# Last image layer and the dense end part with channels on partitions, layers written out on TensorE

## The reference

```python
x = coords @ fc0_w + fc0_b                       # 3 -> 32 channels
for sw, cw, cb in (four layers):
    x1 = spectral_conv(x, sw)                    # rfft2, 20 x 20 modes mixed by sw, irfft2
    x2 = einsum('bchw,oc->bohw', x, cw) + cb     # 1x1 convolution
    x = gelu(x1 + x2)
x = gelu(x @ fc1_w + fc1_b)                      # 32 -> 64 channels, per pixel
return (x @ fc2_w + fc2_b)[..., 0]               # 64 -> 1
```

## Time and profile before

| | |
|---|---|
| median of 3 runs | 4450.04 us (4443.79 to 4450.76) |
| the profiled execution | 4450.9 us, span 4448.7 us |
| mean granted TensorE clock | 0.754 |
| PE busy | 3744.6 us (84%) |
| PEld busy | 3132.7 us (70%) |
| DVE busy | 2504.3 us (56%) |
| ACT busy | 549.9 us (12%) |
| POOL busy | 740.6 us (17%) |
| image block: first transpose of half 1 to last copy into `ho` | 30.0 to 1840.7 us |

### The profile page before, as it was taken

The page is one execution under the profiler, slowest core; times in us unless marked ns, Lnnn a source line. Parts: engine busy times, 40 slices in busy tenths (PEclk is TensorE's granted clock), DMA queues, the critical chain, the costliest instruction groups (busy, mean ns, idle before and its releaser), DMA issues. The chain is left out here.

```text
span 4448.7 us, 109537 instructions
## 1 busy us (share of the span) xinstructions
PE 3744.6 (84%) x44268; PEld 3132.7 (70%) x44268; DVE 2504.3 (56%) x8138; ACT 549.9 (12%) x1173; POOL 740.6 (17%) x1900
## 2 busy tenths in 40 slices
PE   6999999999999999697656566687998878859587
PEld 5898988769989887454424455687997778857444
DVE  4454545145455452223756888888787887852413
ACT  0101011310010112211211110101001000001011
POOL 1000000000000000000002434334343332332021
PEclk9999999999999999777855555555555555556589
DMA  1010000000000000100003110111000000021111
GB/s 37 16 17 2 16 2 16 2 6 16 2 16 16 2 1 2 25 0 4 0 10 91 32 35 29 31 29 31 26 25 32 22 29 24 22 75 46 21 39 27
DMA packets 189736, 96.97 MB, mean 22 GB/s; under 512 B 139463, under 2 KB 172535, under 8 KB 188632
## 3 DMA queue, kind: packets, MB, share of 16 engines
q1 hardware_dynamic: 183574, 84.19, 8.1%
q10 hardware_dynamic: 4626, 7.39, 0.4%
q0 software_dynamic: 1280, 2.10, 0.2%
HBM read 76.11 MB, written 15.96 MB: 21 GB/s over the span
## 5 line engine op out<-in xcount | busy, mean ns | idle before, releaser
L349 PEld LDWEIGHTS im_acc<-im_cwt,im_chan 128*128 128x128 f32 x2048 | 268.7, 191 | 123.0 <-issue 117.3
L468 ACT ACTIVATE im_a<-im_acc 128x512 f32<-128x512 f32 x256 | 152.9, 597 | 1376.7 <-PE im_acc L349 1376.7
L204 POOL DMA_DIRECT2D image_rows<-im_ho x16 | 9.6, 603 | 1761.2 <-DVEq L459 1761.2
L445 DVE COPY im_chan<-im_ring 128x512 f32<-128x512 f32 x192 | 132.8, 692 | 286.8 <-PE im_ring L296 286.8
L346 PE MATMUL im_acc<-im_u,im_e 97*128 97x512 f32 x512 | 265.3, 599 | 7.6 <-DVE im_u L439 7.6
L349 PE MATMUL im_acc<-im_cwt,im_chan 128*128 x2048 | 270.1, 274 | 0.0
L258 PE MATMUL im_ring<-im_d,im_a 128*128 128x128 f32 (+1 forms) x2048 | 242.5, 281 | 19.1 <-issue 12.9
L258 PEld LDWEIGHTS im_ring<-im_d,im_a 128*128 128x128 f32 x2048 | 239.5, 198 | 22.1 <-issue 18.5
L1641 PE MATMUL sc_ps<-H,sc_cols 128*128 128x128 f32 x768 | 231.2, 457 | 11.9 <-POOL H L1528 11.5
L439 DVE COPY im_u<-im_ring 80x512 f32<-80x512 f32 x256 | 171.6, 685 | 118.8 <-PE im_ring L290 118.8
L406 DVE COPY im_half_t<-im_ring 128x480 f32<-128x480 f32 x192 | 168.5, 903 | 116.5 <-PE im_ring L258 116.5
(11 more groups left out here) (394 smaller groups left out, 7460.3 us busy)
## 6 DMA issues: line engine op xcount, KB each, us to landing
sc_g_row<-mem_g_rows_dram SPq DMA_DIRECT2D x96, 256.0 KB, 3.5
im_wbd<-in_c_mix_dram SPq DMA_DIRECT2D x32, 400.0 KB, 6.1
sc_w_row<-mem_w_rows_dram SPq DMA_DIRECT2D x192, 64.0 KB, 2.5
sw_g_all<-sw_gates SPq DMA_DIRECT2D x8, 768.0 KB
mem_hist_h_dram<-sc_hist_h ACTq DMA_DIRECT2D x6, 512.0 KB, 3.0
mem_hist_dz_dram<-sc_hist_dz ACTq DMA_DIRECT2D x6, 512.0 KB, 3.7
mo_hist_dz<-mem_hist_dz_dram SPq DMA_DIRECT2D x8, 384.0 KB, 6.4
mo_hist_h<-mem_hist_h_dram SPq DMA_DIRECT2D x8, 384.0 KB, 6.5
```

The costliest lines, as they stand in the source:

```text
L349: mm = MM(acc[:, p % 2, m:512:4], chan[:, p % 2, m * 128:(m + 1) * 128], cwt[:, bass.ds(l, 1), :].rearrange("p a c -> p (a c)"), start=Fal ...
L468: nc.scalar.activation(a[:, g, :, :].rearrange("p c (w x) -> p (c w) x", x=32)[:, :, p * 4:p * 4 + 4], acc[:, p % 2, :].rearrange("p (c m) ...
```

## The change

- In the last layer of each half (l = 3) the operands of the row inverse swap roles: slices of `u` with a step of 4 are the stationary operand (four times), and the first 128 columns of constants `e2` are the moving one. The convolution swaps too: `cwt[l]` is stationary, `chan` is moving with 512 columns. `acc` then holds channels and column index on partitions, in the layout that the end part needs; ScalarE reads it in the order "(m c)" and writes `a` as before.
- In the end part the transposes, their fills and VectorE's copies are gone. The first dense layer reads `a` itself as moving operand, through an access pattern of 4 x 128 elements in which neighbours are 32 elements apart. `FC_FILLS` goes from 40 to 8.
- On TensorE the loop over the layers is written out in the code, so every wait and address there is a constant. VectorE keeps its loop over four layers. ScalarE loops over three and has the fourth written out.

```diff
-        FC0_FILLS, LAYER_FILLS, FC_FILLS = 4 * 9, 4 * 8 + 10 + 4 * 21, 4 * 10
+        FC0_FILLS, LAYER_FILLS, FC_FILLS = 4 * 9, 4 * 8 + 10 + 4 * 21, 4 * 2
...
-                    with pe.Fori(0, NL) as l:
+                    for l in range(NL):
...
-                                MM(acc[:, p % 2, :], e2[0:97, :], u[:, p, :, :].rearrange("p o w -> p (o w)"), start=True, stop=True, skip_group_check=True)
-                                have(f.base + turned[p])
-                                for m in range(4):
-                                    mm = MM(acc[:, p % 2, m:512:4], chan[:, p % 2, m * 128:(m + 1) * 128],
-                                            cwt[:, bass.ds(l, 1), :].rearrange("p a c -> p (a c)"), start=False, stop=True, skip_group_check=True)
+                                if l == NL - 1:
+                                    for m in range(4):
+                                        MM(acc[:, p % 2, m * 128:(m + 1) * 128], u[:, p, :, :].rearrange("p o w -> p (o w)")[:, m:512:4], e2[0:97, :], start=m == 0, stop=True, skip_group_check=True)
+                                    have(f.base + turned[p])
+                                    mm = MM(acc[:, p % 2, :], cwt[:, l, :], chan[:, p % 2, :], start=False, stop=True, skip_group_check=True)
+                                else:
...
-                            turn_activations(f, g, 4 * q)
                             pend = []
                             for p in range(4):
-                                if p < 3:
-                                    turn_activations(f, g, 4 * q + p + 1)
-                                have(start + p + 1)
+                                pixels = a[:, g, :, :].rearrange("p c (w x) -> p (c w) x", x=32)[:, :, (4 * q + p) * 4:(4 * q + p + 1) * 4].rearrange("p j m -> p m j")
                                 for v in range(2):
...
-                                    MM(acc[:, v, :], fc1[:, v, :], chan[:, p % 2, :], start=True, stop=True).then_inc(acc_full, 1)
+                                    MM(acc[:, v, :], fc1[:, v, :], pixels, start=True, stop=True).then_inc(acc_full, 1)
...
-                            for p in range(4):
-                                V.tensor_copy(chan[:, p % 2, :], drain(f)).then_inc(drained, 1)
...
+                    with act.Fori(0, NL - 1) as l:
+                        layer(l, "p (c m) -> p c m")
+                    layer(NL - 1, "p (m c) -> p c m")
```

More of the change, by code:

```diff
@@ L218, in second_layer @@
                 if p + v == 0:
-                    pe.wait_ge(drained, start + 4 + 1)
+                    pe.wait_ge(drained, start + 1)
                 pe.wait_ge(acc_read, SEEN + n + 1)
@@ L222, in second_layer @@
                     col = v * 32 + p * 4 + m
-                    mm = MM(ring[:, (start + 4) % RING, col:col + 17:16], gl[:, v, m * 128:(m + 1) * 128], fc2[:, :], start=True, stop=True)
+                    mm = MM(ring[:, start % RING, col:col + 17:16], gl[:, v, m * 128:(m + 1) * 128], fc2[:, :], start=True, stop=True)
                 return mm
@@ L345, in _ @@
                                 pe.wait_ge(acc_read, SEEN + n - 1)
-                                MM(acc[:, p % 2, :], e2[0:97, :], u[:, p, :, :].rearrange("p o w -> p (o w)"), start=True, stop=True, skip_group_check=True)
-                                have(f.base + turned[p])
-                                for m in range(4):
-                                    mm = MM(acc[:, p % 2, m:512:4], chan[:, p % 2, m * 128:(m + 1) * 128],
-                                            cwt[:, bass.ds(l, 1), :].rearrange("p a c -> p (a c)"), start=False, stop=True, skip_group_check=True)
+                                if l == NL - 1:
[4 more added lines that the diff above has]
+                                else:
+                                    MM(acc[:, p % 2, :], e2[0:97, :], u[:, p, :, :].rearrange("p o w -> p (o w)"), start=True, stop=True, skip_group_check=True)
+                                    have(f.base + turned[p])
+                                    for m in range(4):
+                                        mm = MM(acc[:, p % 2, m:512:4], chan[:, p % 2, m * 128:(m + 1) * 128], cwt[:, l, :], start=False, stop=True, skip_group_check=True)
                                 mm.then_inc(acc_full, 1)
@@ L463, in _, with layer @@
                 for half in range(2):
-                    with act.Fori(0, NL) as l:
+                    def layer(l, order):
                         for g in range(NGRP):
@@ L467, in _ @@
                                 act.wait_ge(acc_full, half * HALF_ACC + l * LAYER_ACC + g * PH + p + 1)
-                                nc.scalar.activation(a[:, g, :, :].rearrange("p c (w x) -> p (c w) x", x=32)[:, :, p * 4:p * 4 + 4], acc[:, p % 2, :].rearrange("p (c m) -> p c m", m=4), ACT.Gelu).then_inc(acc_read, 1)
+                                nc.scalar.activation(a[:, g, :, :].rearrange("p c (w x) -> p (c w) x", x=32)[:, :, p * 4:p * 4 + 4], acc[:, p % 2, :].rearrange(order, m=4), ACT.Gelu).then_inc(acc_read, 1)
+                    with act.Fori(0, NL - 1) as l:
+                        layer(l, "p (c m) -> p c m")
+                    layer(NL - 1, "p (m c) -> p c m")
                     for n in range(4 * PH * 2):
```

## The result

| | before | after |
|---|---|---|
| median | 4448.35 us (4443.79 to 4450.76, 4 runs) | 4637.98 us (4631.60 to 4646.78, 4 runs) |
| span of the profiled execution | 4448.7 us | 4632.4 us |
| mean granted TensorE clock | 0.754 | 0.723 |

What follows compares the result with a forecast made beforehand. TensorE's own sequence in the image network was taken as the bound. End part -53, written-out layers -26 and strided reads 0 gave -79 us, from 4450 to 4371 us; range 4360 to 4402, main case 4362 to 4380 (64%).

Steps and rivals of the forecast that it cites:

- The strided moving operand, "I take zero": End part's first dense layer: reading with a step of 32 elements costs nothing; upper end +74 us on 256 passes.
- Stride halves the rate: Rival, 8%: each moving pass of the first dense layer takes 0.86 instead of 0.43 us, +110 us, 4481 us.
- `u` with a step of 4 as weights, "I take zero": Last layer's row inverse: strided weight loads stay hidden at no cost; upper end 36 us, by VectorE's factor of 1.68.
- The clock, "1 us left": End parts: of 12 us lost to clock falls at quarter borders, nearly all goes with transposes and wait; 1 us left.
- Clock and fetch stay: Rival, 15%: clock falls come from two-column passes (+11 us) and new code bodies stall when fetched (+13 us): 4380 to 4395.
- Layers written out: TensorE's six layer borders: without the loop's branches 27.3 us of branch and clock loss should go; -26 us taken.
- The swapped roles: Last layer's row inverse and convolution: 1.75 us an item before and after (0.89 + 0.86), no change over 64 items.
- The write of PSUM with a step of 4: Last layer's accumulator: writing without stride instead of with stride 4 was put at zero.
- the gelu's other order: Last layer's gelu on ScalarE: reading PSUM in another order was taken as zero; even twice the time shows only 1.2 us.
- Removing transposes and copies: End parts: sixteen quarters of 14.26 us, 228.2 against 282.06 us; -53.9 us at full clock, -53 us as the term.
- a moving pass over 0.5 us: Sign in the end part's first dense layer: the forecast is wrong if a moving pass takes over 0.5 us.
- the clock in the end parts, the third: Sign in the end parts: the forecast is wrong if the clock still falls at every second border of quarters.

Runs made afterwards that it cites:

- both_wide: Changed kernel with neighbouring elements in both strided reads and 128 instead of 2 moving columns in the second dense layer: 4380.16 us, ratio 0.9834 to the kernel before.
- second_wide: Changed kernel, strided reads kept, with 128 instead of 2 moving columns in the second dense layer: 4545.61 us, ratio 1.0199 to the kernel before.
- turn_plain: Kernel before, its end part's transposes reading 128 neighbouring elements instead of a step of 32: 4459.43 us in a single run, beside 4452.45 for the kernel before.
- before_wide: Kernel before with 128 instead of 2 moving columns in the second dense layer: 4437.31 us, ratio 0.9972 to the kernel before.
- weights_plain: Changed kernel, but the last layer's row inverse loads 128 neighbouring elements as weights instead of a step of 4: 4581.90 us, ratio 1.0285 to the kernel before.
- both_plain: Changed kernel with neighbouring elements in both the first dense layer's read and the row inverse's weights: 4384.78 us, ratio 0.9847 to the kernel before.
- plain_all: Changed kernel without strided TensorE reads, whole computation kept, ScalarE and VectorE writing the needed order: 4380.51 us, ratio 0.9832 to the kernel before.

## Why the prediction was wrong

The forecast was 4371 us, the result 4638: 267 us more. Three terms carry it: 62 us for the strided weights, 106 for the strided moving operand and 98 for the clock, 266 in all by the profiles. The rest cancels (2 us more than forecast in the end parts at full clock, 2 us less at the borders).

**The strided moving operand, "I take zero".** This is the step that failed. At full clock the end parts took 231.24 us with plain reads (both_wide) and 337.02 with strided ones (second_wide): +105.8 us, 0.41 on each of 256 passes. The rival "Stride halves the rate" had the mechanism and the size, 0.43 a pass and +110 us, and got 8%. The argument against it was that a strided transpose load of 128 columns takes 189 ns, like an unstrided load of a two-pass matmul. From it the prediction concluded that a penalty exists, "but one that an f32 pass already pays": a strided element comes every 0.87 ns, a moving pass wants one every 0.84 ns. That step compared loads of two kinds, and it fails: the two don't hide in each other, the stride doubles the f32 pass itself, to 1.66 ns a column (0.85 us/512). A single-pass load of 128 columns without stride, the row that was missing, takes 141 ns (turn_plain). The prediction had that discrepancy in hand as the rival's "for": 71 ns more for 48 columns, where two-pass loads grow by 42. The row of 80 columns of the same kind of pass (118 ns) was the one to compare with. As an estimate from these loads (80 ns fixed, by 141 and 118 ns as by 192 and 150), a column takes 0.48 ns in a plain single-pass load and 0.85 in a strided one, 0.87 in a plain two-pass load and 1.95 in a strided one: each kind is slowed by about two, so a strided load of the first kind looks like a plain one of the second. The trace of before did hold evidence against zero, and the rule on lines of the Trainium skill (Advanced Engine Details and Errata, SBUF Cachelines) pointed the same way; both were weighed as 8%.

**`u` with a step of 4 as weights, "I take zero".** Failed by the same row. Loads grew from 192 to 329 ns, and the passes behind them from 0.111 to 0.233 us: +62 us by the timeline, 56 to 58 by the runs with plain weights. It lay above the upper end of 36 us too, since VectorE's factor of 1.68 on 0.107 us was taken for what is beyond the cover, and TensorE's own factor is 2.1 on the pass (0.233/0.111).

**The clock, "1 us left".** Failed, and in the other direction: the end parts fell to 0.52 and lost 97.7 us. The prediction took the falls to come from the transposes and the wait at each border, so that they would go with these. They need the two-column passes: with these widened and all transposes in place, before_wide holds 1.00 and its end parts are 12.8 us shorter, what the prediction had read off as the old loss (12 us). And taking out transposes and waits doesn't suffice: 5.5 us of loss stay with plain reads, 97.7 with strided ones. The rival "Clock and fetch stay" named the right cause and undersized it, since it didn't join it with the strided read. No rival joined any two terms, though one row (the 189 ns) fed both stride terms.

**The two costs aren't independent.** At the lower level a step takes 3.42 us with and without the stride. With the clock at 1.2 GHz the pass is as slow by itself as the strided read. So 98 us is what the clock takes on top of the stride, and had the clock been low anyway the strided moving operand would have been free.

**What held.** Layers written out: -27.9 us at the borders, forecast 27.3 at most and 26 taken, and no price for new bodies at any border. The swapped roles: 0.89 + 0.86 us an item when the read is plain (weights_plain). The write of PSUM with a step of 4 costs nothing that shows in these passes of 128 columns (0.89 us for eight either way), nor does the gelu's other order (597 ns both times). Removing transposes and copies: 282.06 to 236.78 us in both_plain, -45.3 where 53 was forecast; at full clock on both sides it is 269.30 to 231.24, -38.1, and with the wide second layer as well -50.8. Had both reads been plain, the forecast of -79 us would have stood beside -71 and -74 (both_plain and plain_all, each against the kernel before in its own round).

**What would have shown it**, by the prediction's own list: a moving pass over 0.5 us was the first sign named, and it came; the clock in the end parts, the third, came too, and larger than named.

## What to carry to other kernels

- Before a layout change moves a strided access from one engine's write to TensorE's read, look at whether two neighbours in the stream fall in one 16-byte line: if not, count each such f32 pass, moving or as weights, at twice its time, as here (0.43 to 0.85 us, 0.111 to 0.233). Let the writer that has slack make the order instead.
- Compare a row only with one of the same kind of instruction (single-pass with single-pass), and take a load that is hidden as no evidence for what it costs: read its own duration against a load of the same kind and another size.
- Where one assumption feeds several terms, give the case in which it falls one price for all of them, the clock among them; and where a stream has matmuls with very few columns behind 128-column weights, try more columns, which cost nothing here up to 128.

## What the runs showed of the hardware that was not expected

- At a clock of 1.00 an f32 moving pass of 512 columns takes 0.43 us with neighbours and 0.85 with a step of 32 elements (both_wide, second_wide). Between two-column passes two of them take 0.94 us with neighbours, 0.99 with a step of 2, 1.85 with a step of 4 and 1.77 with a step of 32. An f32 weight load of 128 columns takes 192 ns with neighbours, 196 with a step of 2 and 329 with a step of 4. A transpose's load takes 141 ns with neighbours and 189 with a step of 32.
- The granted clock went down to its lower level while the PE row of the page said 9: TensorE was busy for 216.18 of 216.18 us at a clock of 0.52. Either change, a plain read or a wide second layer, brought it back to 0.97 or 1.00 in the profiled executions; why both together lose it each time wasn't shown.
- With plain reads and two-column passes the clock holds in most executions, but in one of plain_all it went down during the sixteen two-column passes behind the first quarter of an end part and stayed down for the other seven (0.50 over 191 us, each quarter the same). In after it went down in the first end part at the second set of eight two-column passes (816.91 to 818.43, 1.52 us where the first set took 0.82). Why it then stays down, and only in some executions, isn't settled; with 32 or 128 columns no profile shows it.
